# One expert's third weight is split two units later, and a context's values are spread by a 0/1 tile, in a four-layer cross-attention kernel on one core

## Time and profile before

| | before |
|---|---|
| median of 3 runs | 2916.72 us (2914.17 to 2917.75) |
| the profiled execution's own time | 2914.43 us |
| its span | 2912.7 us |
| busy: PE, DVE, ACT, POOL | 82%, 67%, 52%, 28% |
| granted TensorE clock, mean | 0.912 |

### The profile page before, as it was taken

One profiled execution on the slowest core, in us unless ns is written; L12 is line 12 of the kernel. 1 busy time (PEld: TensorE's weight loads), 2 busy tenths in 40 slices (PEclk: granted clock), 3 DMA queues, 4 the chain that ended last, 5 costly groups with the idle time before them and its releaser, 6 DMA issues. The chain is left out here.

```text
span 2912.7 us, 43515 instructions
## 1 busy us (share of the span) xinstructions
PE 2397.6 (82%) x16502; PEld 1969.5 (68%) x16502; DVE 1945.1 (67%) x4389; ACT 1507.7 (52%) x2566; POOL 803.6 (28%) x703
## 2 busy tenths in 40 slices
PE   4778888876689999999859999999999377777765
PEld 3545555554477888888749999999999346464544
DVE  4688878885456666666545666666665457787867
ACT  2456767754445655565434444454444255454534
POOL 2233524432232434444440000000000463525030
PEclk9789889887799999999979999999999688989897
DMA  7500000000000111100024333344332421111000
GB/s 232 220 1 16 16 1 16 8 8 8 32 15 1 43 34 39 34 18 24 20 64 140 120 120 120 127 137 135 120 120 89 140 72 50 55 43 59 1 15 15
DMA packets 152616, 184.22 MB, mean 63 GB/s; under 512 B 21560, under 2 KB 118101, under 8 KB 152408
## 3 DMA queue, kind: packets, MB, share of 16 engines
q1 hardware_dynamic: 139400, 154.16, 16.1%
q0 software_dynamic: 12288, 27.15, 3.0%
q10 hardware_dynamic: 720, 0.12, 0.0%
HBM read 116.38 MB, written 71.43 MB: 64 GB/s over the span
## 5 line engine op out<-in xcount | busy, mean ns | idle before, releaser
L2400 POOL DMA_INDIRECT picked<-expert_out,so x128 | 126.3, 987 | 866.7 <-DMA so<-slots 762.8
L161 PE MATMUL SC<-Xhi,Whi 128*128 128x320 f32 x1024 | 320.1, 313 | 4.3 <-DVE Xlo L2197 2.5
L161 PE MATMUL SC<-Xlo,Whi 128*128 128x320 f32 x1024 | 317.2, 310 | 0.0
L161 PE MATMUL SC<-Xhi,Wlo 128*128 128x320 f32 x1024 | 317.2, 310 | 0.0
L638 POOL TENSOR_TENSOR PR<-PR,rs 128x616 f32<-128x616 f32 x128 | 157.5, 1231 | 400.0 <-DVE rs L1021 399.9
L1405 POOL TENSOR_TENSOR ff_Hlo<-ff_HF,ff_Hhi 128x512 fp32r<-128x512 f32 x108 | 142.8, 1323 | 388.6 <-ACT ff_Hhi L1538 388.5
L2168 ACT ACTIVATE Hhi<-HF 128x320 fp32r<-128x320 f32 x256 | 120.6, 471 | 154.7 <-DVE HF L2223 154.7
L161 PEld LDWEIGHTS SC<-Xhi,Whi 128*128 128x128 f32 x1024 | 193.2, 189 | 4.9 <-issue 2.8
L2211 DVE TENSOR_TENSOR Hlo<-HF,Hhi 128x320 fp32r<-128x320 f32 x256 | 125.5, 490 | 104.2 <-ACT Hhi L2168 104.2
L161 PEld LDWEIGHTS SC<-Xlo,Whi 128*128 128x128 f32 x1024 | 193.2, 189 | 0.0
L161 PEld LDWEIGHTS SC<-Xhi,Wlo 128*128 128x128 f32 x1024 | 193.0, 188 | 0.0
(11 more groups left out here) (490 smaller groups left out, 6954.4 us busy)
## 6 DMA issues: line engine op xcount, KB each, us to landing
expert_in<-zeros SPq DMA_DIRECT2D x4, 5120.0 KB, 32.6
rowsin<-expert_in SPq DMA_DIRECT2D x32, 640.0 KB, 5.9
expert_out<-rowsout SPq DMA_DIRECT2D x32, 640.0 KB, 4.0
first_expert<-L_wg SPq DMA_DIRECT2D x16, 512.0 KB, 6.8
first_expert<-L_wu SPq DMA_DIRECT2D x16, 512.0 KB, 6.8
first_expert<-L_wd SPq DMA_DIRECT2D x16, 512.0 KB, 7.6
Wraw<-L_wg SPq DMA_DIRECT2D x16, 512.0 KB, 6.7
Wraw<-L_wu SPq DMA_DIRECT2D x16, 512.0 KB, 7.1
```

What stands on the lines that cost most here:

```text
L161: last = nc.tensor.matmul(out, lhs[l], rhs[r], start=start and n == 0, stop=stop and n == 2)
L2400: nc.gpsimd.indirect_dma_start(picked[g][:, t, k, :], None, oute[:, :], bass.IndirectOffsetOnAxis(ap=so[g][:, t, k:k + 1], axis=0)).then_i ...
```

## The change

It has four parts.

1. In the experts, the third weight (down) of the next expert is split at unit 3, where PE issues the row transposes, on ACT and on DVE; the first two stay at unit 1, so that `take_output` follows them directly.
2. In the attention stage, the context is multiplied once by both value matrices (`wv`, 256 + 16 columns side by side) into 80 rows, DVE adds the biases (`vctx`), and PE spreads these rows over the 128 rows of each block by a product with a 0/1 tile `spread` (80 x 5 x 128), which POOL makes in the setup by one memset and eight selections. `crep` and `replicate` are gone.
3. ACT copies the spread values out of PSUM (`take_last_values`, `take_values`), in place of DVE; its key copy moves from step 11 to step 12, behind the copy of the transposed rows.
4. `ln_rstd` of `rstd_a` moves on DVE from step 13 to the start of step 14, behind `scale_by_gamma`.

```diff
+        spread = sb("spread", [CTXP, BLK, P])
+        vctx = sb("vctx", [CTXP, D + DH])
...
+                for h in range(HH):
+                    keep_where(spread[:, :, :], [[P, BLK], [1, P]], -CTXP * h, -1, ALU.not_equal, 1.0)
...
-                    def replicate(b):
-                        if b:
-                            act.wait_ge(ctx_in, 16 * b)
-                            act.wait_ge(v_psum, b)
-                        nc.scalar.activation(crep[:, :, :, :], bc_at(ctxT[:, :, :], 2, HH), ACT.Copy).then_inc(crep_ready, 1)
...
+                    def take_last_values(b):
+                        act.wait_ge(v4_psum, b + 1)
+                        if b:
+                            act.wait_ge(vbd0_ready, b)
+                        if b >= 2:
+                            act.wait_ge(kv1_ready, b - 1)
+                        nc.scalar.activation(vtmp[:, BLK - 1, :], wide[:, TOK:TOK + D], ACT.Copy)
+                        nc.scalar.activation(v1tmp[b % 2][:, :, :], wide[:, V1AT:V1AT + BLK * DH].rearrange("p (j d) -> p j d", d=DH), ACT.Copy)\
+                            .then_inc(v4_taken, 1)
+
+                    def take_values(b):
+                        act.wait_ge(v_psum, b + 1)
+                        nc.scalar.activation(vtmp[:, 0:BLK - 1, :], wide[:, :].rearrange("p (j d) -> p j d", d=D), ACT.Copy).then_inc(v_taken, 1)
...
-                            if s == (0 if c == 0 else 10) and c is not None:
-                                replicate(c)
...
-                            if s == (1 if c == 0 else 11) and c is not None:
-                                take_keys(c)
...
+                            if s == (2 if c == 0 else 12) and c is not None:
+                                take_keys(c)
+                            if s == (3 if c == 0 else 13) and c is not None:
+                                take_last_values(c)
+                            if s == (5 if c == 0 else 15) and c is not None:
+                                take_values(c)
...
                     def keys(b):
-                        pe.wait_ge(crep_ready, b + 1)
+                        if b:
+                            pe.wait_ge(ctx_in, 16 * b)
...
+                        for k in range(KC):
+                            last = nc.tensor.matmul(wide[0:CTXP, TOK:TOK + D + DH], ctxT[:, k, :], wv[:, k, :], start=k == 0, stop=k == KC - 1)
+                        last.then_inc(k_psum, 1)
+
+                    def last_values(b):
+                        pe.wait_ge(vctx_ready, b + 1)
+                        nc.tensor.matmul(wide[:, TOK:TOK + D], spread[:, BLK - 1, :], vctx[:, 0:D], start=True, stop=True)
                         for j in range(BLK):
...
+                            last = nc.tensor.matmul(wide[:, V1AT + j * DH:V1AT + (j + 1) * DH], spread[:, j, :], vctx[:, D:], start=True, stop=True)
+                        last.then_inc(v4_psum, 1)
+
+                    def values(b):
+                        pe.wait_ge(kcol_ready, b + 1)
+                        pe.wait_ge(v4_taken, b + 1)
+                        for j in range(BLK - 1):
+                            last = nc.tensor.matmul(wide[:, j * D:(j + 1) * D], spread[:, j, :], vctx[:, 0:D], start=True, stop=True)
+                        last.then_inc(v_psum, 1)
...
-                            if s == (4 if c == 0 else 12) and c is not None:
-                                pe.wait_ge(kcol_ready, c + 1)
-                                values(0, BLK // 2)
+                            if s == (3 if c == 0 else 12) and c is not None:
+                                last_values(c)
                             if s == (4 if c == 0 else 14) and c is not None:
-                                pe.wait_ge(v4_taken, 2 * (c + 1))
-                                values(BLK // 2, BLK - 1).then_inc(v_psum, 1)
+                                values(c)
...
+                    def add_value_bias(b):
+                        dve.wait_ge(k_psum, b + 1)
                         if b:
...
+                            dve.wait_ge(v_psum, b)
+                        tt(vctx[:, :], wide[0:CTXP, TOK:TOK + D + DH], bvr[:, :], ALU.add).then_inc(vctx_ready, 1)
...
+                            if s == 14 and 0 <= h < NH:
+                                ln_rstd(h, LN["a"], var_a, sd_a, rstd_a)
                             if now is not None:
                                 shift(now)
...
-                            if s == 13 and 0 <= h < NH:
-                                ln_rstd(h, LN["a"], var_a, sd_a, rstd_a)
...
                             if u == DOWN_AT and j + 1 < E2:
-                                for n in range(NW):
+                                for n in range(2):
                                     weights_high(j + 1, n)
+                            if u == ROWS_AT and j + 1 < E2:
+                                weights_high(j + 1, 2)
...
                             if u == DOWN_AT:
                                 if j + 1 < E2:
-                                    for n in range(NW):
+                                    for n in range(2):
                                         weights_low(j + 1, n)
                                 if j:
                                     take_output(j - 1)
+                            if u == ROWS_AT and j + 1 < E2:
+                                weights_low(j + 1, 2)
```

More of the change, by code:

```diff
@@ L378, in attention_layers @@
         router1, route2, iota32, count, ctxT, before, onesb = (W[n] for n in ("router1", "route2", "iota32", "count", "ctxT", "before", "onesb"))
-        wq0, wk0, wv0, wo0 = (sb(n, [P, KC, D]) for n in ("wq0", "wk0", "wv0", "wo0"))
+        wq0, wk0, wo0 = (sb(n, [P, KC, D]) for n in ("wq0", "wk0", "wo0"))
         wq1, wo1 = (sb(n, [P, KC, D]) for n in ("wq1", "wo1"))
-        wk1, wv1 = sb("wk1", [P, KC, DH]), sb("wv1", [P, KC, DH])
+        wk1, wv = sb("wk1", [P, KC, DH]), sb("wv", [P, KC, D + DH])
         wk1r = sb("wk1r", [P, KC, HH, DH])
@@ L395, in attention_layers @@
         bk1c, cb1c = sb("bk1c", [P, 1]), sb("cb1c", [CH, 1])
-        bv0r, bo0r, bo1r, gammar, betar = (sb(n, [P, D]) for n in ("bv0r", "bo0r", "bo1r", "gammar", "betar"))
-        bv1r, cb2r, knotr, tempr, oscr = sb("bv1r", [P, DH]), sb("cb2r", [P, 2]), sb("knotr", [P, KNOTS]), sb("tempr", [P, 1]), sb("oscr", [P, 1])
+        bo0r, bo1r, gammar, betar = (sb(n, [P, D]) for n in ("bo0r", "bo1r", "gammar", "betar"))
+        bvr, cb2r, knotr, tempr, oscr = sb("bvr", [CTXP, D + DH]), sb("cb2r", [P, 2]), sb("knotr", [P, KNOTS]), sb("tempr", [P, 1]), sb("oscr", [P, 1])
         negt = sb("negt", [P, 1])
@@ L451, in attention_layers @@
                 (cb1c, a["L0_cb1"].rearrange("(p a) -> p a", a=1)),
[L452 to L453 removed]
+                (bvr[:, 0:D], rows(a["L0_bv"], CTXP)), (bo0r, rows(a["L0_bo"])), (bo1r, rows(a["L1_bo"])),
+                (gammar, rows(a["L0_gamma"])), (betar, rows(a["L0_beta"])), (bvr[:, D:], rows(a["L1_bv"], CTXP)), (cb2r, rows(a["L0_cb2"])),
                 (knotr, rows(a["L0_knots"])), (tempr, rows(a["L0_temp"])), (oscr, rows(a["L0_osc"])),
@@ L879, in unit_transposes @@
                         last.then_inc(pt_psum, 1)
-                    def rep(j, k):
-                        return crep[:, k, :, :].rearrange("p h c -> p (h c)")[:, j * P:(j + 1) * P]
                     def keys(b):
-                        pe.wait_ge(crep_ready, b + 1)
+                        if b:
+                            pe.wait_ge(ctx_in, 16 * b)
                         for c in range(KC):
@@ L891, in keys @@
                                              start=k == 0, stop=k == KC - 1)
-                        for j in range(BLK):
-                            for k in range(KC):
-                                nc.tensor.matmul(wide[:, V1AT + j * DH:V1AT + (j + 1) * DH], rep(j, k), wv1[:, k, :], start=k == 0, stop=k == KC - 1)
-                        for k in range(KC):
-                            last = nc.tensor.matmul(wide[:, TOK:TOK + D], rep(BLK - 1, k), wv0[:, k, :], start=k == 0, stop=k == KC - 1)
-                        last.then_inc(k_psum, 1)
-                    def values(j0, j1):
-                        for j in range(j0, j1):
-                            for k in range(KC):
-                                last = nc.tensor.matmul(wide[:, j * D:(j + 1) * D], rep(j, k), wv0[:, k, :], start=k == 0, stop=k == KC - 1)
-                        return last
+                        for k in range(KC):
[4 more added lines that the diff above has]
+                        nc.tensor.matmul(wide[:, TOK:TOK + D], spread[:, BLK - 1, :], vctx[:, 0:D], start=True, stop=True)
+                        for j in range(BLK):
+                            last = nc.tensor.matmul(wide[:, V1AT + j * DH:V1AT + (j + 1) * DH], spread[:, j, :], vctx[:, D:], start=True, stop=True)
[6 more added lines that the diff above has]
+                        last.then_inc(v_psum, 1)
                     def signatures(h):
@@ L1171, in _ @@
```

(2 more changed lines are left out.)

29 lines of the change are left out of this document (9 added, 20 removed).

## The result

| | before | changed |
|---|---|---|
| median | 2916.88 us (2914.17 to 2917.75) | 2890.13 us (2885.63 to 2894.47), 4 runs |
| ratio | | 0.9912, interval 0.9901 to 0.9924 |
| the profiled execution | 2914.43 us, span 2912.7 | 2885.63 us, span 2883.9 |

The change makes the kernel 26.8 us faster. The forecast was 2882 us (2868 to 2899): the side was right, the size 8 us too large. Timed again beside the experiments, the changed kernel took 2888.15 us, 29.8 less than before.

A forecast was written before the change was run, and what follows sets the result against it. PE was taken to bound the experts, a braid of short PE and DVE chains the attention stage. Terms 18.0 + 1.1 + 3.6 + 7.2 + 0 + 5.0 = 34.9 us off 2914.43 gave 2879.5, forecast 2882 us (2868 to 2899).

The forecast's parts named there:

- The wait at the transposes goes whole: Experts: PE's wait for DVE's down-product copy vanishes, 30 x 0.60 = 18.0 us, plus 1.1 us in the first expert.
- Unit 6 costed at nothing: Experts: HF comes later but slack falls only from 0.5 to 0.1 us; no cost, or up to 6 us if it fails.
- Setup hidden: Setup: POOL's eight selections cost 3 to 13 us but finish by 20 us, before PE's first instruction at 23.31.
- First context: Attention start: first scores 5.6 us sooner, less 2 us for the lower PE clock; gain 3.6 us (-1.6 to 5.6).
- Contexts: Halves 2 and 4: fewer PE passes and ACT's earlier rows and PT copy gain 3.6 us net each, 7.2 us.
- the braid eats it: Halves 2 and 4: low case of the gain, only 1 us each, against 5.3 for the whole.
- Half 0: Attention: PE gains 1.9 us up to the projection but then waits for ACT's copies; gain 0, between -1 and 1.5.
- ACT's value copies as what PT waits for: Attention: sign of being wrong, ACT's value copies appearing as what PE's signatures or PT wait for; no size given.
- rstd_a behind gamma: Halves 1, 3, 5, 6, 7: gamma fills DVE's wait for the root, about 1.0 us each, 5.0 us (0 to 8).
- under 0.5: Attention: sign of being right, gamma ahead of rstd_a on DVE with the wait under 0.5 us.
- the attention stage gives little: Attention: PE gaps keep 1.2 GHz, waits move to ACT; 0 to 5 us there, 2893 to 2898 us total; chance 0.14.
- ACT's copies, 0.5 us more in each context by a page's rule: Attention: the page's ScalarE budget gives 1.15 us per 1024 columns, 0.5 us more in four contexts; the trace shows 1.02.

The follow-up runs named there:

- e1: The kernel before with only the third expert weight's split moved to unit 3: 2898.17 us beside 2917.18, ratio 0.9936.
- e8: The changed kernel with the third weight's split one unit later, at unit 4: 2913.97 us, ratio 0.9989 to the kernel before.
- e5: The changed kernel run again, same program, as the measure for runs beside it: 2888.15 us, ratio 0.9896 to the kernel before.
- e6: The changed kernel with ACT's key copy back in step 11 (step 1 for the first context), ahead of the row copies: 2895.88 us.
- e2: The kernel before with only ln_rstd of rstd_a moved to the start of step 14: 2918.72 us, ratio 1.0004.
- e11: The changed kernel with rstd_a ahead of gamma as before, second run of this version: 2887.09 us, ratio 0.9896 to the kernel before.
- e10: The changed kernel with three more DVE memsets in the setup ahead of PE's first instruction: 2887.57 us, ratio 0.9905 to the kernel before.
- e3: The changed kernel with the expert split and the rstd_a move undone, leaving the spread values and ACT copies: 2904.54 us, ratio 0.9956 to the kernel before.
- e12: The changed kernel with the value copies on DVE instead of ACT, run again: 2877.13 us, ratio 0.9871 to the kernel before.
- e7: The changed kernel with the spread values copied by DVE in steps 13 and 15 instead of ACT: 2881.11 us, ratio 0.9879 to the kernel before.
- e9: The changed kernel with the value copies on DVE and rstd_a back ahead of gamma: 2882.86 us, ratio 0.9876 to the kernel before.
- e4: The changed kernel with rstd_a back in step 13, ahead of gamma, first run: 2883.32 us, ratio 0.9890 to the kernel before.

## Why the prediction was right, and where not

**The wait at the transposes goes whole, 18.0 + 1.1: right.** The stage shrank by 19.4 us and e1 alone by 19.0. The reading that made it right was to take the pitch between matmuls (0.75 less 0.15 us) and not the bracket of 0.45. The first expert gave 3.07 - 1.94 = 1.1 us.

**Unit 6 costed at nothing, with 0.1 us of slack: right.** The slack was 0.3 us. e8 gives it its price: past the point, 0.8 us an expert.

**Setup hidden: right.** Eight selections took 6.96 us, 0.87 each, between my bounds; POOL is done by 14.1 us, PE starts at 23.34.

**First context, 3.6: under-sized, 5.1, with some luck in it.** I had 5.6 less 2.0 for a projection partly at 1.2 GHz. The loss was 5.40 - 3.70 = 1.7 us, and the projection began at 33.97 rather than 34.8, since the transposes of XP already ran at 2.4 GHz (1.10 us for eight; they took 1.89 before). In e5 they did not (1.97), the projection began at 34.87, as forecast, and the scores came at 44.41. I had read the 1.2 GHz of the kernel before from durations alone; its record of the granted clock starts only at 40.1 us, so that the profile's 1.00 ahead of it says nothing.

**Contexts, 3.6 each: under-sized, 4.8 and 5.2.** The path was the right one, with ACT's key copy as its main step (e6). I took a value between "the braid eats it" and the whole; the measured one is close to the whole, less the two waits behind ACT's copies. Half 0 (forecast 0) gave 1.7. A sign that I had named for being wrong came true here, ACT's value copies as what PT waits for: it cost part of the gain and did not turn it.

**rstd_a behind gamma, 5.0: this step failed.** It was 0 as far as the runs can tell (e2, e11 against e10), and DVE's wait in half 3 was 0.80 us where I had named "under 0.5" as the sign of being right. I took DVE's wait as time of the stage: "gamma fills the first wait and POOL gets its input sooner: about 1.0 us in each". I followed the gain to POOL and no further. The question I did not ask is who waits for DVE there: PE's scores did come sooner, but PE then stood waiting for ACT's PT by the same amount, and `rstd_c`, for whose root DVE now waits longer, took up the rest.

**A cost that was not in the sum.** Halves 1, 3 and 5 lose 0.9, 1.8 and 1.3 us. In half 3 it is seen at the output projection of layer 0. Before:

```profile
299.63 0.79 PE L180 MATMUL SC<-Kbd,QT 64*128 64x308 f32 x4
...
301.42 3.72 PE L847 MATMUL GP<-wo,OT 128*128 128x256 f32 x16
```

and in the changed kernel:

```profile
289.01 1.40 PE L180 MATMUL SC<-Kbd,QT 64*128 64x308 f32 x4
...
291.35 4.83 PE L860 MATMUL GP<-wo,OT 128*128 128x256 f32 x16
```

The scores ahead of it take 1.40 us, which is 1.2 GHz (a granted clock of 0.50), where they took 0.79; the projection takes 1.1 us more for the same 16 passes. It does so in every other kernel with the spread part but one (4.77 to 4.98 us in e3 to e8 and e10 to e12) and neither in e1 nor in e2 (3.72): it comes with the spread part. The same projection in half 5 takes 3.72 us in the kernel before, e1 and e2, 4.60 to 4.80 with the spread part, and 3.83 and 3.95 in e7 and e12. The exception is e9, whose first HG came at 108.6 us: 3.72 us in half 3, and a half of 77.3, but 4.95 in half 5. Half 3 from mark to mark reads, before, changed and in e7:

```profile
255.92:332.42 76.50, 62.02 (x520) 39.56 (x520) 68.25 (x161) 54.16 (x92) 34.00 (x28) 0.91 0.05 16
```
```profile
245.12:323.38 78.26, 65.43 (x522) 41.33 (x520) 68.67 (x162) 54.27 (x92) 35.06 (x28) 0.87 0.05 16
```
```profile
244.80:323.11 78.31, 66.01 (x524) 41.55 (x524) 68.68 (x162) 54.29 (x91) 35.09 (x28) 0.87 0.05 16
```

PE is busy 3.4 us longer in the changed kernel for the same work, at a lower granted clock, and the copies on DVE do not bring that back in this half. My rival "the attention stage gives little" named this mechanism (gaps that keep PE at 1.2 GHz, waits that move to ACT) and gave it 0.14. It was right as a mechanism, and much smaller: it took about 4 us, or 7 with half 7, where the rival had 11 to 16. What stays open is why the spread part changes the clock of a half that it does not touch. No run here kept PE from its gaps in such a half, and none shows which gap decides.

**ACT's copies, 0.5 us more in each context by a page's rule.** The rule was that of the Trainium skill, page "ScalarE: Activation LUTs", section "Rules for kernel authors", adds to VectorE. It speaks of adds, and what ACT took over is a plain copy. The copy itself was cheap, as the trace had said (1.02 us). Yet the placement cost 4 to 7 us (e7 beside e5, e9 beside e11), so VectorE was the better place, for a reason that is not the price per element. About 2 us of it are shown, in the two halves with a context, where PT and PE stand behind the copy; for the rest, in other halves, no run shows the cause.

**Sum by its own terms.** Forecast 34.9: experts 19.1, first context 3.6, contexts 7.2, swap and half 0 5.0. Measured in the marks: 19.4, 5.1, 10.0, and 1.7 - 7.4 = -5.7. That the total came so near is in part luck: the terms that were too small (5.1 for 3.6, 10.0 for 7.2, 1.7 for 0) made up for about half of the one that failed and the cost that was missing. The profiled execution is 28.8 us shorter; its own time 2885.63 is the lowest of four, which is why the medians differ by 26.8 only.

## What to carry to other kernels

A wait on an engine that others wait for is worth its length only if nothing else holds the engine it feeds: follow a gain to the next engine that has to be released, here PE, and add up all that PE waits for there before and after. Where one engine is full (the experts), a wait measured by pitch can be counted to a tenth of a microsecond; where three engines are braided, look first for the copy that others queue behind, since its place (3.5 us a context for the key copies) can matter more than its length (0.54 and 0.34 us). And ask of each step that is moved how far it could go before it costs: here one unit further took back 24 us.

## What the runs showed of the hardware that I had not expected

- The granted clock follows the schedule in some stretches and not in others. Shifting everything by 2 us (e10) left the length of every half the same to 0.3 us, low stretches and all. But in the first context one and the same program had its XP transposes at 2.4 GHz in one execution (1.10 us) and at 1.2 GHz in the next (1.97 us, e5).
- Half 7 has two lengths, 75.7 to 76.3 and 79.2 to 79.9 us. The kernel before had the short one in its profile, while e1 and e2, which have the same instructions in this stage up to the swap, had the long one; with the spread part e4, e7 and e12 had the short one. A single profile of a braided stage can so mislead by 3 us.
- Two executions of one and the same program (e7, e12) reached the end of half 0 at 104.4 and 101.1 us, and then agreed to 0.3 us in every half.
- A selection over 640 columns took 0.87 us on POOL, 3.1 times one of 128 columns (0.28 us).
